# Attention, dense layer and routed GEGLU in one kernel: a later down product, routing weights side by side, and ScalarE, VectorE and GpSimd in another order where attention ends

## The reference, cut to what matters

```
x = x + xattn(layernorm(x), ctx)     # two attention layers, then a dense layer
    a = attention(x, x);    x = layernorm(x + a) * g1 + b1       # 16 heads of 64
    a = attention(x, ctx);  x = layernorm(x + a) * g2 + b2
    h = gelu(x @ fc1 + c1)                                       # 256 -> 1024
    x = layernorm(x + h @ fc2 + c2) * g3 + b3                    # 1024 -> 256
x = x + ffn(layernorm(x))
    shared = (gelu(x @ w1s) * (x @ w2s)) @ w3s                   # 256 -> 1024 -> 256
    e = argmax(x @ Wg)                                           # 8 experts, top 1
    final = (gelu(x @ W1[e]) * (x @ W2[e])) @ W3[e]
    return shared + final
```

## Time and profile before

| | |
|---|---|
| median of three runs | 1266.42 us |
| the profiled execution | 1266.5 us |
| its span | 1264.8 us |
| PE busy | 1225.6 us, 97% |
| DVE busy | 993.7 us, 79% |
| ACT busy | 878.3 us, 69% |
| POOL busy | 707.2 us, 56% |
| chain that ended last | PE 78%, DVE 11%, ACT 5% |

### The profile page before, as it was taken

The page is one execution under the profiler, slowest core; times in us unless marked ns, Lnnn a source line. Parts: engine busy times, 40 slices in busy tenths (PEclk is TensorE's granted clock), DMA queues, the critical chain, the costliest instruction groups (busy, mean ns, idle before and its releaser), DMA issues.

```text
span 1264.8 us, 31447 instructions
## 1 busy us (share of the span) xinstructions
PE 1225.6 (97%) x10447; PEld 1170.8 (93%) x10447; DVE 993.7 (79%) x2680; ACT 878.3 (69%) x2261; POOL 707.2 (56%) x1104
## 2 busy tenths in 40 slices
PE   7899999999999999999999998999999999999998
PEld 5899999999999999999999997999999999998898
DVE  6898888888899988888888897445455888888864
ACT  5778788888878888888888875444224667777642
POOL 4766656656678756556656678786333223333351
PEclk9999999999999999999999999999999999999999
DMA  6060000000000005000000100010023777777722
GB/s 192 2 242 19 12 8 18 18 2 18 27 2 26 27 2 193 27 2 26 27 2 27 35 2 26 28 49 27 1 97 122 236 246 248 236 238 246 252 93 81
DMA packets 74383, 100.60 MB, mean 80 GB/s; under 512 B 5616, under 2 KB 53616, under 8 KB 74224
## 3 DMA queue, kind: packets, MB, share of 16 engines
q1 hardware_dynamic: 72688, 94.40, 22.6%
q0 software_dynamic: 1536, 4.20, 1.0%
HBM read 84.16 MB, written 14.42 MB: 78 GB/s over the span
## 4 chain that ended last, share of the span: by engine, by line
PE 78%; DVE 11%; ACT 5%; issue 4%; POOL 2%; DMA 0%; DVEq 0%; ACTq 0%; POOLq 0%
PE ps_pj L52 9%; PE ps_pj L54 9%; PE ps_pj L53 9%; PE ps_t L946 8%; PE ps_s L936 8%; PE ps_pv L959 7%; PE ps_aux L52 3%; PE ps_aux L54 3%; PE ps_aux L53 3%; ACT probs L1261 3%; PE ps_s L52 3%; PE ps_s L54 3%; PE ps_s L53 3%; PE ps_pv L52 2%; PE ps_pv L53 2%
## 5 line engine op out<-in xcount | busy, mean ns | idle before, releaser
L664 POOL TENSOR_SCALAR probs<-probs,inv 128x256 f32<-128x256 f32 x512 | 236.9, 483 | 224.5 <-DVE inv L1495 223.8
L1261 ACT ACTIVATE probs<-scores,nb 128x256 f32<-128x256 f32 x512 | 253.6, 497 | 19.5 <-DVE nb L1485 19.0
L1485 DVE CUSTOM_DVE_ANT_0 scores<-ps_s,maskf 128x256 f32<-128x256 f32 x512 | 186.7, 420 | 51.5 <-PE ps_s L936 49.3
L1268 ACT ACTIVATE probs_t_hi<-ps_t 128x512 fp32r<-128x512 f32 x256 | 150.9, 590 | 105.4 <-PE ps_t L946 105.4
L1499 DVE TENSOR_TENSOR probs_t_lo<-ps_t,probs_t_hi 128x512 fp32r<-128x512 f32 x256 | 172.8, 675 | 1.4 <-ACT probs_t_hi L1268 1.3
L946 PE MATMUL ps_t<-ident,probs 128*128 128x128 f32 x1024 | 140.0, 279 | 0.6 <-POOL probs L664 0.6
L959 PE MATMUL ps_pv<-probs_t_lo,v_stack 128*128 128x256 f32 x512 | 130.3, 287 | 0.7 <-issue 0.7
L959 PE MATMUL ps_pv<-probs_t_hi,v_stack 128*128 128x256 f32 x512 | 127.6, 282 | 0.0
L946 PEld LDWEIGHTS ps_t<-ident,probs 128*128 128x128 f32 x1024 | 109.7, 141 | 17.9 <-POOL probs L664 0.9
L52 PE MATMUL ps_pj<-xq_hi,wq_lo 128*128 128x256 f32 x368 | 115.3, 313 | 4.3 <-POOL wk_lo L711 4.2
L683 POOL TENSOR_TENSOR heads_t_lo<-joined,heads_t_hi 128x256 fp32r<-128x256 f32 x128 | 94.9, 741 | 35.1 <-ACT heads_t_hi L1277 34.7
(11 more groups left out here) (284 smaller groups left out, 4553.1 us busy)
## 6 DMA issues: line engine op xcount, KB each, us to landing
raw<-in_L_ffn_W SPq DMA_DIRECT2D x96, 512.0 KB, 5.6
slot_rows<-hin SPq DMA_DIRECT2D x3, 768.0 KB, 5.8
rows<-in_x SPq DMA_DIRECT2D x8, 256.0 KB, 2.7
after_self<-rows SPq DMA_DIRECT2D x8, 256.0 KB, 2.9
rows<-after_self SPq DMA_DIRECT2D x8, 256.0 KB, 2.7
cin<-in_ctx SPq DMA_DIRECT2D x8, 256.0 KB, 3.1
after_cross<-rows SPq DMA_DIRECT2D x8, 256.0 KB, 2.1
stage<-in_L_xattn_fc_w SPq DMA_DIRECT2D x2, 1024.0 KB, 9.2
```

What stands on the lines that cost most here:

```text
L664: last = pool.tensor_scalar(PR[:, h, t, :], PR[:, h, t, :], inv[:, h, t:t + 1], 1.0, ALU.mult, ALU.mult)
L1261: last = act.activation(PR[:, h, t, :], SM[:, h, t, :], ACT.Exp, bias=nb[:, h, t:t + 1], scale=-1.0, accum_out=sums[:, h, t:t + 1])
L1268: act.activation(flat(PT[0][:, i % 2, h, :, :]), ps_t[h][:, :], ACT.Copy).then_inc(t_hi, 1)
L1485: last = dve.tensor_tensor_reduce(SM[:, h, t, :], ps_s[h][:, t * S:(t + 1) * S], maskf[:, i // PAIRS % 2, :], -SCALE, -LOWEST, ALU.add, AL ...
```

## The change

Four things are changed.

1. `down_single(step - 1, 1)` is issued one block later: in a pair or shared step after the second up and gate products instead of after the first, in a single after its second up product instead of before it. In pair and shared steps VectorE's `finish` of that single moves from behind the first gate to behind the second.
2. The high and low halves of Wg lie side by side. Per row tile and half of the width, one matmul takes the low rows against Wg's high half (8 columns) and one the high rows against both halves (16 columns). `choose` adds the two groups of 8 in one more VectorE instruction.
3. Where attention ends, ScalarE takes `gelu_dense(0)` and `hi_of_pair(125)` before the last probabilities and `gelu_dense(1)` before `hi_of_pair(127)`. VectorE takes the high halves of pieces q3, o0 and o1 before the last probabilities, and the last residual sum, piece o3, the last output statistics and the shared pieces' high halves between and behind the hidden low halves of step 0.
4. The low halves of the four shared pieces move from GpSimd, behind `norm_second(0)`, to VectorE, in step 1 between the first and the second hidden low half (`shared_lows`), with a semaphore of their own. GpSimd takes `finish_dense(n)` before `bias_rows(n + 1)`.

```diff
@@ -120,7 +120,7 @@
              {0: [("q", 0)], 1: [("k", 0), ("v", 0)], 2: [("q", 1), ("k", 1)], 3: [("v", 1)],
-              6: [("q", 2), ("q", 3)], 7: [("o", 0), ("o", 1)], 9: [("o", 2)], 11: [("o", 3)],
+              6: [("q", 2)], 7: [("q", 3), ("o", 0)], 8: [("o", 1)], 9: [("o", 2)], 11: [("o", 3)],
               12: [("k", 2), ("v", 2), ("k", 3), ("v", 3)]}]
@@ -134,6 +134,7 @@
 LATE_SECOND = sum(1 for piece in LATE if piece[0] <= 1)
+SHARED_PIECES = PIECES_AT[NPAIR + 4]

@@ -315,7 +316,7 @@
         b1 = little("b1", [P, FC])
-        WG, wg_raw = (little("wg_hi", [P, KC * E], F32R), little("wg_lo", [P, KC * E], F32R)), little("wg_raw", [P, KC, E])
+        WG, wg_raw = little("wg", [P, KC, 2, E], F32R), little("wg_raw", [P, KC, E])
         position, slot_expert = little("position", [P, TT], I32), little("slot_expert", [P, SLOTS], I32)
@@ -364,6 +365,7 @@
         w3_in, w3_hi, w3_lo = sem("w3_in"), sem("w3_hi"), sem("w3_lo")
+        shared_lo = sem("shared_lo")
         early_hi, early_lo, late_hi, late_lo = sem("early_hi"), sem("early_lo"), sem("late_hi"), sem("late_lo")
@@ -839,21 +841,22 @@
             lo_of_pair(NPAIR - 2)
+            split_late(NPAIR)
             lo_of_pair(NPAIR - 1)
-            for i in range(NPAIR, NPAIR + 4):
+            for i in range(NPAIR + 1, NPAIR + 4):
                 split_late(i)
...
             for n in range(DENSE):
+                if n + 1 == DENSE:
+                    routing_constants()
+                finish_dense(n)
                 if n + 1 < DENSE:
                     bias_rows(n + 1)
-                else:
-                    routing_constants()
-                finish_dense(n)
+                if n == 1:
+                    pool.wait_ge(shared_lo, len(SHARED_PIECES))
                 norm_second(n)
-                if n == 0:
-                    split_late(NPAIR + 4)
             count_tiles()
@@ -1002,17 +1005,20 @@
                 for t in range(ST):
+                    col = (2 * n + t) * 2 * E
                     for c in range(KC):
-                        col = (2 * n + t) * E
-                        last = product(pe, ps_l[:, col:col + E], tuple(x[:, c, t * P:(t + 1) * P] for x in XQ[1]),
-                                       tuple(w[:, c * E:(c + 1) * E] for w in WG), n == 0 and t == 0 and c == 0, c == KC - 1)
+                        hi, lo = (x[:, c, t * P:(t + 1) * P] for x in XQ[1])
+                        pe.matmul(ps_l[:, col:col + E], lo, WG[:, c, 0, :], start=n == 0 and t == 0 and c == 0, stop=False,
+                                  skip_group_check=True)
+                        last = pe.matmul(ps_l[:, col:col + 2 * E], hi, WG[:, c, :, :].rearrange("p k e -> p (k e)"), start=False,
+                                         stop=c == KC - 1, skip_group_check=True)
                 last.then_inc(logits_done, 1)
...
                 for k, stationary in enumerate((lower, ones)):
-                    last = pe.matmul(ps_l[:, (k + 1) * TT * E:(k + 2) * TT * E], stationary[:, :], chosen_flat, start=True, stop=True,
+                    last = pe.matmul(ps_l[:, (k + 2) * TT * E:(k + 3) * TT * E], stationary[:, :], chosen_flat, start=True, stop=True,
                                      skip_group_check=True)
@@ -1066,7 +1072,8 @@
                     if load < 0:
-                        pe.wait_ge(late_lo, len(LATE))
+                        pe.wait_ge(late_lo, len(LATE) - len(SHARED_PIECES))
+                        pe.wait_ge(shared_lo, len(SHARED_PIECES))
                 later = 2 * j if one else j // 2 * 2
@@ -1189,9 +1196,9 @@
                     up_gate(step, 0)
+                    up_glu(step, 1)
                     if after_single:
                         down_single(step - 1, 1)
-                    up_glu(step, 1)
                     turn_gated(step, 0)
@@ -1204,7 +1211,7 @@
                         up_gate(step, j)
-                        if j == 0 and after_single:
+                        if j == 1 and after_single:
                             down_single(step - 1, 1)
@@ -1275,6 +1282,16 @@
 +            def gelu_dense(e):
...

@@ -1297,6 +1314,9 @@
                         hi_of_bank(extra)
+                    if i == NPAIR - 1:
+                        gelu_dense(0)
+                        hi_of_pair(i - 2)
                     hi_of_probs(i, 0)
@@ -1306,23 +1326,13 @@
                     hi_of_bank(extra)
-                if i >= 2:
+                if 2 <= i < NPAIR - 1:
                     hi_of_pair(i - 2)
...
                     act.wait_ge(wg_in, 16)
-                    act.activation(WG[0][:, :], flat(wg_raw[:, :, :]), ACT.Copy).then_inc(wg_split, 1)
-
-            def gelu_dense(e):
...
+                    act.activation(WG[:, :, 0, :], wg_raw[:, :, :], ACT.Copy).then_inc(wg_split, 1)

@@ -1366,8 +1376,8 @@
             hi_of_pair(NPAIR - 2)
-            gelu_dense(0)
             cross_of_pair(NPAIR - 1)
+            gelu_dense(1)
             hi_of_pair(NPAIR - 1)
@@ -1377,7 +1387,8 @@
                     for j in range(1, HP):
-                        gelu_dense(e + j)
+                        if e + j > 1:
+                            gelu_dense(e + j)
                         hi_dense(e + j - 1)
@@ -1420,7 +1431,7 @@
                     act.wait_ge(counted, 1)
-                    act.activation(counts[:, :, :, :].rearrange("p k t e -> p (k t e)"), ps_l[:, TT * E:3 * TT * E], ACT.Copy)\
+                    act.activation(counts[:, :, :, :].rearrange("p k t e -> p (k t e)"), ps_l[:, 2 * TT * E:4 * TT * E], ACT.Copy)\
                         .then_inc(counts_ready, 1)
@@ -1455,6 +1466,12 @@
                     dve.tensor_copy(piece(W[kind][0], 0, kind, q), raw_piece(kind, q)).then_inc(late_hi, 1)
+
+            def shared_lows():
+                for kind, q in SHARED_PIECES:
+                    dve.wait_ge(late_hi, LATE_COUNT[(2, kind, q)])
+                    dve.tensor_tensor(piece(W[kind][1], 0, kind, q), raw_piece(kind, q), piece(W[kind][0], 0, kind, q).bitcast(F32),
+                                      ALU.subtract).then_inc(shared_lo, 1)

@@ -1612,7 +1629,9 @@
                 dve.wait_ge(constants_ready, 1)
-                link(dve.tensor_copy(logits[:, :, :].rearrange("p t e -> p (t e)"), ps_l[:, 0:TT * E]))
+                both = ps_l[:, 0:2 * TT * E].rearrange("p (t k e) -> p t k e", k=2, e=E)
+                link(dve.tensor_copy(logits[:, :, :], both[:, :, 0, :]))
+                link(dve.tensor_tensor(logits[:, :, :], both[:, :, 1, :], logits[:, :, :], ALU.add))
                 link(dve.tensor_reduce(top[:, :], logits[:, :, :], AX.X, ALU.max))
@@ -1688,6 +1707,9 @@
                     lo_of_bank(("qk", i + 2))
+                if i == NPAIR - 1:
+                    late_hi_pieces(i)
+                    late_hi_pieces(i + 1)
                 lo_of_probs(i, 0)
@@ -1696,10 +1718,11 @@
                     lo_of_bank(extra)
-                late_hi_pieces(i)
+                if i < NPAIR - 1:
+                    late_hi_pieces(i)
                 if i == 2 * PAIRS:
                     dve.wait_ge(wg_split, 1)
-                    dve.tensor_tensor(WG[1][:, :], flat(wg_raw[:, :, :]), WG[0][:, :].bitcast(F32), ALU.subtract).then_inc(wg_split, 1)
+                    dve.tensor_tensor(WG[:, :, 1, :], wg_raw[:, :, :], WG[:, :, 0, :].bitcast(F32), ALU.subtract).then_inc(wg_split, 1)
                 if p == 2 and u >= 1:
@@ -1710,10 +1733,6 @@
             lo_of_hidden(0, 0)
-            residual_sum(NTURN - 1)
-            late_hi_pieces(NPAIR + 3)
-            output_stats(NTURN - 1)
-            late_hi_pieces(NPAIR + 4)
             for step in range(STEPS):
@@ -1725,9 +1744,17 @@
                         lo_of_hidden(step, 0)
+                    if step == 1:
+                        shared_lows()
                     for j in range(1, HP):
                         lo_of_hidden(step, j)
+                        if step == 0 and j == 1:
+                            residual_sum(NTURN - 1)
+                            late_hi_pieces(NPAIR + 3)
                     lo_of_x(("x", step + 1))
+                    if step == 0:
+                        output_stats(NTURN - 1)
+                        late_hi_pieces(NPAIR + 4)
                     if step >= 1:
@@ -1757,8 +1784,6 @@
                 gate(step, 0)
-                if is_single(step - 1):
-                    finish(step - 1)
                 if step == DENSE:
@@ -1770,6 +1795,8 @@
                     gate(step, j)
+                    if j == 1 and is_single(step - 1):
+                        finish(step - 1)
                     if splits:
```

More of the change, by code:

```diff
@@ L1277, in hi_of_pair, with gelu_dense @@
                 act.activation(OT[0][:, i % 4, :], joined[:, i % 2, :], ACT.Copy).then_inc(o_hi, 1)
+            def gelu_dense(e):
+                n, j = e // HP, e % HP
+                if e == 0:
+                    act.wait_ge(tail_in, 16 * 4)
+                act.wait_ge(du_done, e + 1)
```

(4 more changed lines are left out.)

8 lines of the change are left out of this document (removed).

## The result

The changed kernel takes 1245.3 us, median of four runs (1244.4 to 1246.9), against 1266.7 for the kernel before in the same series (1264.8 to 1267.4): ratio 0.9835, 95% interval 0.9818 to 0.9852. In a later series its five runs had a median of 1245.8 (1242.6 to 1246.2; ratio 0.9829, 0.9815 to 0.9843). 1242 was predicted, with a range of 1237 to 1253. The profiled execution took 1244.4, its span is 1242.6: 22.2 us less than before, where 24.2 were predicted.

What follows compares the result with a forecast made beforehand. TensorE, busy 97% of the 1264.8 us span, was taken as the bound, so gains came from its waits, slow clock and matmul count. 7.0 + 1.6 + 3.6 + 12.0 = 24.2 off 1266.5 gave 1242, range 1237 to 1253.

Steps and rivals of the forecast that it cites:

- Part 1, to step 1: Attention into dense: reordering removes the 4.6 us wait and low clock; the down product ends at 785.2, 8.7 us sooner.
- 1.38 us of drain: ScalarE's table load before the last probabilities: counted in addition, attend(127) comes 1.4 later and part 1 gives 5.6; not adopted.
- Part 1, in step 1: Hidden low halves behind statistics and shared_lows: 0.2 and 1.5 us lost, leaving part 1 at 7.0, ends 2.5 and 8.7.
- second rival: Boundary into dense stalls 4.9 us, low clock costs 2.7 again; part 1 gives 0.9, total 1248; chance 0.15.
- Part 1b: Steps 2 and 3: normed(1) wait of 1.5 and 0.1 refill goes, GpSimd's other order costs nothing; 1.6, ends 0 and 1.6.
- Part 2: Routing logits, eight batches: 32 fewer matmuls at 0.11 us, 16 columns costing what 8 do; 3.6 us gained.
- Part 3: Later down product, seven pair steps and shared step 29: 8 x 1.54 less 0.3 for margins, 12.0; ends 0 and 12.9.
- The single after a single: Step 28, the ninth wait: PE would wait for DVE's gate until the same 1201.33, so nothing gained.
- The tail: Kernel's end: gathers start 2 us later, once; added rows are wanted later still, so nothing lost, 1 at most.
- The first: Rival: DVE becomes the bound in the pair steps; 1248, or 1254 if all is given back; chance 0.17, 0.04 at 1254.
- the third: Rival: normed rows stay late (1.6) and 16 columns cost double (3.6); 1247; chance 0.09.
- The fourth: Rival: late finish holds raw loads behind store_slot, PE waits for weights in each pair step; 1270; chance 0.03.

Runs made afterwards that it cites:

- e9_edge_tuned: Changed kernel with shared low halves moved to steps 2 and 4, GpSimd's first norm before bias rows, third weights' low halves in step 5: 1241.07 us, ratio 0.9799.
- e4_finish_back: Changed kernel with VectorE's finish of a single back behind the first gate: 1253.26 us, ratio 0.9898.
- e3_edge_only: Changed kernel without the later down product and the side-by-side routing weights: 1261.87 us, ratio 0.9958 to the kernel before.
- e8_ss_gate: Changed kernel with step 28's gate ahead of the last two low halves VectorE owes from step 27: 1245.7 us in one execution.
- e11_changed_again: The changed kernel, unaltered, run again as reference in a later series: 1245.76 us, ratio 0.9829 to the kernel before.
- e6_lows_later: Changed kernel with all four shared low halves moved from step 1 to step 2: 1244.6 us in one execution.
- e5_casts_late: Kernel before with only VectorE's last output statistics and four shared high halves moved behind step 0's hidden low halves and the next batch's rows: 1263.0 us, ratio 0.9974.
- e7_norm_first: Changed kernel with GpSimd norming batch 0's rows before it adds bias_rows(1): 1244.5 us in one execution.
- e10_tail_tuned: e9_edge_tuned with additions of gathered rows moved to the ends of steps 29 and 30 and into step 31: 1241.33 us, ratio 0.9804 to the kernel before.

## Why the prediction was right, step by step

**Part 1, to step 1.** Predicted 8.7; measured 8.57, or 8.97 against the first landmark. The table load has its gelu directly behind it again:

```profile
768.70 1.28 ACT L1293 ACT_TABLE_LOAD   x1 [0.30 <-PE ps_s L54]
769.99 0.81 ACT L1293 ACTIVATE ps_s<-ps_s,b 128x256 f32<-128x256 f32 x2
...
771.03 1.09 ACT L1275 ACTIVATE probs_t_hi<-ps_t 128x512 fp32r<-128x512 f32 x2
```

The copies started at 771.03 where 770.8 was predicted, and attend(127) at 773.80 where 773.5 was. That decided for the row and against the 1.38 us of drain that the Trainium skill (ScalarE: Activation LUTs, What ACT_TABLE_LOAD costs) would have added: part 1 did not shrink by 1.4.

**Part 1, in step 1.** Predicted 0.2 + 1.5 lost (the 0.2 has no working: the prediction has both the low half and PE at 791.4); measured 1.64, one wait of 1.30 and its refill. DVE's rows:

```profile
789.85 0.75 DVE L1537 BATCH_NORM_STATS2 part<-hin 128x6 f32<-128x256 f32 x2 [3.61 <-POOL rows L699]
...
791.37 0.68 DVE L1473 TENSOR_TENSOR wk_lo<-stage,wk_hi 128x512 fp32r<-128x512 f32 x1
...
793.18 0.69 DVE L1473 TENSOR_TENSOR wv_lo<-stage,wv_hi 128x512 fp32r<-128x512 f32 x1
793.78 0.68 DVE L1564 TENSOR_TENSOR gt_lo<-ps_s,gt_hi 128x512 fp32r<-128x512 f32 x1
```

`y_ready` came at 789.85, for 789.7 predicted, and the four subtractions (the two in the middle are left out here) started 0.60 apart, 2.4 us, the cheap end of the bounds. The prediction's low end for part 1, 2.5, does not come out of its own terms: a wait of 4.9 leaves 3.6, and 0.9 with the low clock, as its second rival has it.

**Part 1b failed, the one step that did.** Predicted: GpSimd's other order costs nothing, `normed(0)` at 801.6 where PE wants it at 801.8. Measured: 2.06 us of waiting for it, until 803.98. GpSimd's rows:

```profile
792.73 2.02 POOL L675 TENSOR_SCALAR hin<-hin,nmean,rstd 128x256 f32<-128x256 f32 x2
...
798.71 1.75 POOL L727 TENSOR_TENSOR xin<-xin,beta_b 128x512 f32<-128x512 f32 x1
...
801.74 1.02 POOL L673 TENSOR_TENSOR rstd<-veps,mhalf 128x2 f32<-128x2 f32 x1
```

Beside `shared_lows` the norm of `finish_dense(0)` takes 2.02 for 1.10 (all of `finish_dense(0)` 6.5 for 5.2), while DVE's subtractions keep their 0.60: there GpSimd alone paid. Beside the four low halves of w3 both pay: `bias_rows(1)` takes 1.75 for 1.29, the small steps of the norm 1.02 for 0.70, and DVE's four 3.71 us at 798.50, where the earlier trace rows has 2.46. In e9_edge_tuned, where DVE's subtractions stand elsewhere, GpSimd's are back at the lower figures. The last part was to be read before the change: the kernel before has the same norm beside the same low halves, from here to 807.62, 3.4 us, and the prediction gave it 2.5 (799.1 to 801.6).

```profile
804.17 0.54 POOL L669 TENSOR_SCALAR veps<-mv 128x2 f32<-128x2 f32 x1 [2.98 <-DVE mv L1523]
...
806.52 1.10 POOL L673 TENSOR_SCALAR stage<-stage,nmean,rstd 128x256 f32<-128x256 f32 x2
```

So `normed(0)` came 2.4 us later than worked out: 1.3 in `finish_dense(0)`, 0.5 in `bias_rows(1)`, 0.9 in the norm, less 0.3 because the chain started sooner. The prediction had costed the contention for DVE alone; the chain that it had put at a margin of 0.2 stood on the other side of the same port. The Trainium skill (SBUF - State Buffer, Who interferes with whom) has the exclusion of two such instructions; here, beside `shared_lows`, the loser was GpSimd (6.5 us for 5.2). The 1.5 us wait for `normed(1)` went as predicted, 1.7 with its refill. By step 4 part 1 and 1b had given 7.3 + 0.4 against the first landmark, less 0.9 that is the logits': 6.8, not 8.6.

**Part 2.** Predicted 3.6; measured 0.45 a batch, 8 x 0.45 = 3.6. Both shapes are 0.11 apart, as the weight loads beside them are.

**Part 3.** Predicted 1.54 x 8 less 0.3 for margins, 12.0; measured 1.61 x 7 to step 27 and 1.6 in step 29, 12.8. The margins held; a wait takes its refill with it, so the upper end was right. DVE in step 14:

```profile
990.73 0.68 DVE L1572 TENSOR_TENSOR ps_s<-ps_s,gelu 128x512 f32<-128x512 f32 x1
991.33 0.41 DVE L1612 COPY hin<-ps_aux 128x256 f32<-128x256 f32 x1
991.66 1.28 DVE L1583 TENSOR_TENSOR wo_lo<-raw,wo_hi 128x512 fp32r<-128x512 f32 x2
```

The copy finds its product done. The single after a single gained nothing, as worked out: its two waits of 1.40 at L1540 and 0.24 at L1555 are now one of 1.63 at 1180.12. The tail was put at nothing, 1 at most: 0.7. DVE stands for a gather ahead of the 0.43 us wait at 1228.95:

```profile
1225.55 0.69 DVE L1676 TENSOR_TENSOR stage<-stage,found 128x512 f32<-128x512 f32 x1 [2.27 <-DMA found<-slot_out,position]
```

**The sum.** Against 24.2: +0.3 at the boundary, -0.4 for an attention that ended later, +0.1 in step 1, -2.3 for `normed(0)`, +0.1 for `normed(1)`, +0.8 in part 3, -0.7 in the tail: 22.1; the spans differ by 22.2. So 1.3 of unforeseen gain hides 3.4 of unforeseen loss. The time fell in the range because part 1b, though wrong, was small; that the total is within 2.1 owes part to luck.

**The rivals.** The first (DVE as bound in the pair steps) did not come; e4_finish_back shows the waits it would have had. The second came in small, at another place: not 4.9 us behind `shared_lows` but 2.06 behind GpSimd, with the low clock in one of the two profiles of the changed kernel. That accounts for most of the distance from 1242 to 1245.3. Of the third neither half came: the wait for `normed(1)` went, and 16 columns cost what 8 do. The fourth did not show: PE has no listed wait at all between 985 and 1175.

## What to carry to other kernels

When work is moved from one of VectorE and GpSimd to the other, cost both engines' chains in that stretch, the one that lost the work too, and put the moved instructions where the other engine's chain has slack, not just where their own has. A wait removed gives its idle time and about 0.2 us of refill; when a product is moved later, the instruction that waits for it has to move as far: left behind, it took 8 of the 12.8 us back. Before a wait is called harmless by its length, look at the granted clock behind it in more than one execution, and look at the waits that the change leaves alone too: here one at 46 us moves the whole kernel by up to 2.7 us from execution to execution.

## What the runs showed of the hardware

**A wait of 1 to 3 us is a lottery.** The kernels here gave PE a wait for normed rows in steps 2 and 3 of many executions. After 2.06 us the clock stayed at 1.00 once (the changed kernel's first profile) and fell four times (e3_edge_only, e4_finish_back, e8_ss_gate, e11_changed_again, readings of 0.52 to 0.91 in the 3 us windows behind it); after 2.29 (e6_lows_later) and 2.51 (e5_casts_late) it fell; after 1.30, 1.79 and 1.98 it read 1.00 each time. A fall cost about 1.5 us. I had expected it only behind waits such as the 4.6. Length alone does not tell: the wait of 1.1 us that ends near 26 us in all 13 profiles has two of 0.6 ahead of it, and behind it the clock fell in five of the 13 profiles (0.66 from 25 to 30 us in the changed kernel's) and read 1.00 in e4_finish_back.

**Attention's end moves with the clock near its start.** The first landmark stood between 762.24 and 765.03 in the 13 profiles. All 13 have a wait of 2.9 us (2.86 to 2.96) that ends near 46 us. In two, e4_finish_back and e5_casts_late, the clock stayed at 1.00 behind it, and from the end of the wait to the first landmark it took 715.6 us in both. In the other eleven it fell: 716.8 to 717.2 us in eight, 718.2 to 718.3 in the three with the lowest readings (e3_edge_only, e7_norm_first, e9_edge_tuned). Most of the difference is there within 6 us of the wait, and it stays to the end of attention. The windows from 45 to 50 us, first of e4_finish_back, then of e9_edge_tuned:

```profile
45.00:50.00 5.00, 3.41 (x29) 3.44 (x30) 3.10 (x11) 2.86 (x10) 3.18 (x6) 1.00 0.00 0
...
45.00:50.00 5.00, 3.39 (x16) 3.42 (x17) 2.05 (x9) 2.25 (x9) 3.19 (x6) 0.55 0.00 0
```

These two places together are about as large as the spread of the changed kernel, 1242.6 to 1246.9 over nine runs, of which only two were profiled. From the transposes in step 14 to those in step 29 the changed kernel, its repetition, e9_edge_tuned and e10_tail_tuned took 201.89, 201.90, 201.88 and 201.88 us, so terms below 1 us are to be read from a stretch of the trace and not from the medians.
